# Local attention's last turns: the next stage's statistics and powers two turns later, the last low half ahead of the last residual

## The reference

```
x = x + retention_block(layernorm(x))      # two layers of retention and feed-forward
x = x + ternary_ffn(layernorm(x))
x = x + local_attention(layernorm(x))      # 16 query heads, 4 key heads, window 64
x = x + ternary_ffn(layernorm(x))
```

```
rms = sqrt(sum(x * x)) / sqrt(d)
x_norm = x / (rms + EPS)
```

## Time and profile before

| | |
|---|---|
| Median of 3 runs | 1459.81 us (1459.66 to 1461.78) |
| Profiled execution, its own time | 1459.51 us |
| Its span | 1457.6 us |
| Busy, share of the span | TensorE 96%, VectorE 73%, ScalarE 64%, GpSimd 55% |
| Mean granted clock of TensorE | 0.994 |
| Last turns of local attention and handover | about 1271 to 1308 us |

### The profile page before, as it was taken

How to read it: one execution, slowest core, us unless ns; L and a number is a source line. 1 busy time by engine, 2 the same in 40 slices (tenths; PEclk the granted TensorE clock), 3 DMA queues, 4 the chain that set the end, 5 groups by cost and what they waited for, 6 DMA issues and landing times. The chain is left out here.

```text
span 1457.6 us, 36349 instructions
## 1 busy us (share of the span) xinstructions
PE 1405.6 (96%) x13004; PEld 1169.9 (80%) x13004; DVE 1059.7 (73%) x2347; ACT 927.1 (64%) x1872; POOL 809.0 (55%) x884
## 2 busy tenths in 40 slices
PE   6999999999998999999999999998899999989998
PEld 5777877889896788888889888887677777768886
DVE  6877777565546887776664669775899999966775
ACT  4665565565552655555655558776778887767775
POOL 3766666322113657665552437776666666636774
PEclk9999999999999999999999999999999999999999
DMA  7000000100001000000311010000000000000101
GB/s 228 31 2 1 0 1 2 37 1 1 1 1 58 2 2 1 0 2 2 103 43 29 1 41 1 1 0 1 2 2 0 0 0 0 0 2 10 36 29 44
DMA packets 21176, 26.28 MB, mean 18 GB/s; under 512 B 1984, under 2 KB 19136, under 8 KB 20928
## 3 DMA queue, kind: packets, MB, share of 16 engines
q1 hardware_dynamic: 20768, 24.61, 5.2%
q10 hardware_dynamic: 288, 0.07, 0.0%
HBM read 20.48 MB, written 4.19 MB: 17 GB/s over the span
## 5 line engine op out<-in xcount | busy, mean ns | idle before, releaser
L548 DVE TENSOR_TENSOR ffn_h_lo<-ffn_h,ffn_h_hi 128x512 fp32r<-128x512 f32 x112 | 86.2, 770 | 122.2 <-ACT ffn_h_hi L759 122.2
L758 ACT ACTIVATE ffn_h<-ffn_hp,c_b 128x512 f32<-128x512 f32 x112 | 77.3, 690 | 145.2 <-PE ffn_hp L857 144.7
L548 DVE TENSOR_TENSOR ternary_ffn_h_lo<-ternary_ffn_h,ternary_ffn_h_hi 128x512 fp32r<-128x512 f32 x128 | 110.8, 865 | 76.4 <-ACT ternary_ffn_h_hi L759 76.3
L2218 POOL TENSOR_TENSOR win_rms<-win_sq_sum,win_minus_half 128x20 f32<-128x20 f32 x31 | 109.8, 3540 | 65.0 <-DVE win_sq_sum L2333 65.0
L1253 POOL TENSOR_TENSOR ret_qk<-ret_qk,ret_qk_sin 128x512 f32<-128x512 f32 x64 | 82.7, 1292 | 99.4 <-DVE ret_qk_sin L1360 98.7
L870 PE MATMUL ternary_ffn_yp<-down_ternary,ternary_ffn_h_hi 128*128 128x256 f32 x512 | 132.4, 291 | 0.0
L870 PE MATMUL ternary_ffn_yp<-down_ternary,ternary_ffn_h_lo 128*128 128x256 f32 x512 | 127.7, 282 | 0.0
L870 PE MATMUL ffn_yp<-down_hi,ffn_h_hi 128*128 128x256 f32 x448 | 127.5, 285 | 0.0
L1259 POOL TENSOR_TENSOR ret_rstd<-ret_sums,ret_minus_half 128x16 f32<-128x16 f32 x32 | 103.7, 3240 | 42.7 <-DVE ret_sums L1402 42.7
L870 PE MATMUL ffn_yp<-down_hi,ffn_h_lo 128*128 128x256 f32 x448 | 125.0, 279 | 0.0
L870 PE MATMUL ffn_yp<-down_lo,ffn_h_hi 128*128 128x256 f32 x448 | 125.0, 279 | 0.0
(11 more groups left out here) (331 smaller groups left out, 4683.0 us busy)
## 6 DMA issues: line engine op xcount, KB each, us to landing
staging<-in_w SPq DMA_DIRECT2D x4, 1024.0 KB, 6.1
ffn_x_in<-in_x SPq DMA_DIRECT2D x8, 512.0 KB, 3.7
X<-in_x SPq DMA_DIRECT2D x7, 512.0 KB, 8.0
out<-X SPq DMA_DIRECT2D x7, 512.0 KB, 2.9
staging<-in_wqkv SPq DMA_DIRECT2D x2, 768.0 KB, 4.5
rotary<-in_rotary SPq DMA_DIRECT2D x1, 1024.0 KB, 6.8
staging<-in_w_up SPq DMA_DIRECT2D x1, 1024.0 KB, 5.1
staging<-in_w_down SPq DMA_DIRECT2D x1, 1024.0 KB, 7.6
```

Of the source, the lines that this page charges most:

```text
L548: nc.vector.tensor_tensor(h_lo[:, m % R, :], h[:, m % R, :], h_hi[:, m % R, :].bitcast(F32), ALU.subtract).then_inc(h_ready, 1)
L758: nc.scalar.activation(h[:, m % R, :], hp[m % 2][:, :], fn, bias=bias)
L2218: nc.gpsimd.tensor_tensor(rms[:, 1, :], sq_sum[:, :], minus_half[:, :], ALU.pow).then_inc(rms_work, 1)
```

## The change

On VectorE, the eight statistics were five at the end of turn 32 and three with the aggregation at the end of turn 33. Now two stand at the end of turn 33, two in turn 34 between the last `row_max` and the probability copy, and four with the aggregation at the end of turn 34. `next_normalise` moves from the end of turn 34 to the end of turn 35. On GpSimd, `next_scales` moves from the end of turn 33 to the end of turn 34. On TensorE, in turn 36, `next_transposes(0)` moves from the front to behind `weighted` and `out_product`. On VectorE, in turn 37, `next_input_low(1)` moves from behind the last `residual` to ahead of it. No operation is added or left out.

```
--- before.py
+++ after.py
@@ -2243,7 +2243,7 @@
                         head_scales(n - 2)
                     if fresh(n):
                         norm_scale(n, k)
-                    if isinstance(n, int) and n == NT + 1:
+                    if isinstance(n, int) and n == NT + 2:
                         next_scales()
 
             skewed(pool, body, N, first=2, last=2)
@@ -2413,6 +2413,8 @@
                         output_low(n - 6)
                     if live(n - 4, NT):
                         row_max(n - 4, 2)
+                    if isinstance(n, int) and n == NT + 2:
+                        next_statistics(range(2, 4))
                     if live(n - 2, NT) and not made(n - 2, 1):
                         square_sums(n - 2)
                     if live(n - 2, NT) and not made(n - 2, 3):
@@ -2430,18 +2432,18 @@
                     if final_tile(n - 4):
                         probs_copy(n - 4, 1)
                         divide(n - 5, k - 5)
+                    if isinstance(n, int) and n == NT + 5:
+                        next_input_low(1)
                     if live(n - 6, NT):
                         residual(n - 6, i, k, 6)
                     if live(n - 2, NT) and not made(n - 2, 1):
                         rotary_sum(n - 2)
-                    if isinstance(n, int) and n == NT + 5:
-                        next_input_low(1)
-                    if isinstance(n, int) and n == NT:
-                        next_statistics(range(0, 5))
                     if isinstance(n, int) and n == NT + 1:
-                        next_statistics(range(5, 2 * TB))
+                        next_statistics(range(0, 2))
+                    if isinstance(n, int) and n == NT + 2:
+                        next_statistics(range(4, 2 * TB))
                         next_aggregate()
-                    if isinstance(n, int) and n == NT + 2:
+                    if isinstance(n, int) and n == NT + 3:
                         next_normalise()
 
             skewed(dve, body, N, first=2, last=2)
@@ -2712,9 +2714,9 @@
                     n = U * i + k
                     here, past, six = (live(n - lag, NT) for lag in (4, 5, 6))
                     if final_tile(n - 5):
-                        next_transposes(0)
                         weighted(n - 5, k - 5)
                         out_product(n - 6)
+                        next_transposes(0)
                         transpose_back(n - 5)
                         next_transposes(1)
                         continue
```

## The result

The changed kernel took 1457.07 us (median of 16 runs, 1456.10 to 1458.54), the kernel before 1459.88 (16 runs): a ratio of 0.9981 with a 95% interval of 0.9975 to 0.9988, 2.8 us less, and 1.75 to 3.65 by the interval. Forecast were 1456.4, with 1454.0 to 1459.4 as the range. Two later comparisons gave 0.9985 (0.9975 to 0.9995) and 0.9987 (0.9978 to 0.9996).

The account below looks back on a forecast made before the run. TensorE, busy 96% of the span, was taken as the bound: 1459.51 - 2.2 (two waits) + 0.64 (late low half) + 0.53 (transpositions) - 0.60 (last low half) - 1.4 (clock) = 1456.4 us, range 1454.0 to 1459.4.

Parts of the forecast that it names:

- The two waits: TensorE's waits before the key transpositions of turns 33 (1.13 us) and 34 (1.08 us) both go: 2.2 us earlier.
- Two statistics ahead of the probability copy: Turn 34, VectorE: the copy comes 0.2 us late, taken as hidden (0); bare, it would cost 0.2.
- The powers: GpSimd, turn 34: start at 1289.4, scales ready at 1295.5, last value copies at 1296.55, 0.3 us to spare.
- Rival D: Powers on GpSimd become the bound, value copies late, slower than before; 1462.6 us if 5.0 late; chance 0.06.
- Rival E: Only one of the two waits goes, head scales or scores ending last in turn 34: 1459.0 us; chance 0.06.
- Turn 36: TensorE's output product stalls 1.15 us for `output_low` behind four normalisations; with transpositions 0.53, 1.2 of 2.2 us are spent.
- The last low half: Stage end, VectorE: it fits into the wait for the last product, so the stage ends 0.60 us earlier.
- The sum without the clock: Shift of the handover to the last feed-forward stage from the work alone: 1.64 us earlier, time 1457.9 us.
- The clock: TensorE after the handover: the 6.8 us low stretch costs 3.1 us; shortened to 3.4, 1.4 us come back.
- case C: No fall of TensorE's clock at the handover, all 3.1 us regained: 1454.8 us; chance 0.26.
- rival A: The clock behaves as before, 6.8 us low after the handover; only 1.64 us gained: 1457.9 us; chance 0.26.
- B: The low stretch after the handover is halved: 1456.4 us, the forecast itself; chance 0.36.

Follow-up runs that it names:

- the doubled power: Changed kernel with one power on GpSimd done twice (the same value), against the kernel before: ratio 0.9989 (0.9980 to 0.9999), way 41.48 us.

## Why the prediction came out as it did

- *The two waits* (2.2 us). Right: both are gone, and the key transposition of turn 34 comes 17.25 us after that of turn 32 instead of 19.54, 2.29 less.
- *Two statistics ahead of the probability copy* (0). Right: in before's clock time the copy starts at 1286.05, 0.1 us late against a shift of 2.2 (forecast 0.2), and `transpose_back` of this turn is still 2.3 us earlier than before. The way needs no term for it.
- *The powers.* In before's clock time (0.51 later) GpSimd starts at 1289.36, forecast 1289.4; the copies end at 1296.42, forecast 1296.55; the weighted product starts at 1296.84, forecast 1296.86. Rival D stayed away with a margin of 0.4 us, and the doubled power shows how it would begin. Rival E stayed away as closely as forecast: the head scales of turn 34 end at 1281.32 (forecast 1281.4) and `pad` starts at 1281.72 (forecast 1281.75).
- *Turn 36.* The stall was right in place and too large: 0.92 us, forecast 1.15. The output product starts at 1298.84 in before's clock time, forecast 1299.02, because the residual ahead of the four normalisations comes 0.11 earlier than worked out (1296.73) and they hold the queue 1.29 us and not 1.36. The transpositions behind it cost 0.43 (1299.15 to 1299.58), forecast 0.53.
- *The last low half* (0.60). Right: 0.58 alone, 0.58 between the changed kernel and the one without it.
- *The sum without the clock.* Forecast 1.64 us, measured 1.92; the difference is the 0.1 of the waits and the 0.2 of turn 36.
- *The clock*, the step that was mis-sized: "which at 2.4 GHz would have taken half, so the low stretch cost 3.1". It costs 1.97 us of tail, and a stretch of half the length 1.1 to 1.2 less than the whole one, not 1.4. At full clock the matmuls do not take quite half as long, and they run into ScalarE. The ground for case C, that 2.38 us of idle time leave the clock alone, was the exception among the profiles. And the forecast put the gain of a shorter stretch into the predicted time as if it belonged to the change. The three profiles of the changed kernel have 6.8, 3.4 and 6.8 us, the two of before 6.8 and 6.8. By rival A, with 1.92 in place of 1.64, the time is 1459.88 - 1.92 = 1457.96, a ratio of 0.9987. All three intervals hold it. The three ratios leave between 0 and 0.9 us for the clock. Whether the shorter gap at the handover (2.02 us in place of 2.60) makes the long stretch rarer is not settled by so few profiles. A and B are both seen, in different launches of the changed kernel; C in none.

So the time came out inside the range in part by luck. The range, 5.4 us wide, held every case from C to E, and two errors offset each other: the shift of the work was put 0.28 us too low, and the clock's 1.4 us, which one launch of three shows and then as 1.1, stood for something between 0 and 0.9. (The terms of the sum add up to 1456.48, which was written as 1456.4.) What bears the prediction out is the way, which the profiles repeat to 0.01 us, with both waits gone and the new stall where it was forecast.

The sentence of the Trainium skill on run-to-run variation (TensorE: Matmul & The Clock Gate, Part 1) speaks of the start of a kernel. Here the like is seen within the launch: three launches of the changed kernel had low stretches in different places and of different lengths, and their times differ with it. The two unequal stretches that the prediction set beside it stood in one launch and could not yet show that. The sum that books only the shift of the way to the change, 1457.9, and the one with a shorter stretch, 1456.4, lie on either side of the measured 1457.07, 0.8 and 0.7 away.

## What to carry to other kernels

Work for the next stage that is tucked into the last turns of this one was free only behind the instruction for which the bounding engine waits. Ask of each piece what stands behind it in the queue, and move it past that; then look where it lands, since here 1.0 of the 2.3 us won were given back two turns later by the normalisations in front of an output half. Where several stages hand over with a gap of TensorE of about 2 us, measure between two instructions of one profile and not from launch to launch, and try a few extra transpositions in the idle time ahead: here twelve of them were worth 1.6 us beside the 1.9 by which the change shortens the way.

## What the hardware showed unexpectedly

Gaps of 2.0 and 2.6 us at the last handover were followed by a low stretch in all twelve profiles, of 6.8 or 3.4 us, and a gap of 2.72 us within local attention by one too. The gap of 2.38 us before the first ternary stage was followed by one in 12 profiles of 14, and that of 2.47 us at the start of the second retention layer in 7 of 14. So neither a fall nor its length follows from the gap alone. With a gap of 1.53 or 1.58 us at the last handover and the idle time ahead of it filled, none came. The low clock cost 1.97 us for 6.8 us, less than a half: the matmuls start every 0.23 us in place of 0.43, and ScalarE is the next bound.
